# Narrow products of a decoder kernel padded to all 128 rows, and expert choice beside the scan split in two

## What is computed

```python
x = x + _L0_attn_ref(ln(x), ...)         # a scan over the 16 entries
x = x + _L0_xattn_ref(ln(x), ctx, mask)  # 16 heads of 8, 77 context rows
x = x + _L0_ffn_ref(ln(x), ...)          # router, top 2 of 8 experts, FF 512
x = x + _L1_attn_ref(ln(x), ...)         # self-attention with ALiBi
x = x + _L1_xattn_ref(ln(x), ctx, ctx, mask2, ...)
x = x + _L1_ffn_ref(ln(x), ...)          # top 2 of 8 again
```

```python
def step(params, x):
    z, y = x @ t_k.T, x @ t_v.T
    grads = grad(loss)(params, z, y)
    new = params - LR * grads
    return new, recon(new, x @ t_q.T)    # z + gelu(z W1' + b1) W2' + b2
```

## Time and profile before

| | |
|---|---|
| time, three runs | 741.73, 746.4, 748.1 us (median 746.4) |
| profiled execution | 753.57 us, of it a span of 751.5 us from first to last instruction |
| instructions | 18475 |
| PE busy | 603.6 us (80% of the span) |
| DVE, ACT, POOL busy | 483.9, 431.8, 359.0 us |
| granted TensorE clock, mean | 0.848 |

### The profile page before, as it was taken

One profiled execution on the slowest core, in us unless ns is written; L12 is line 12 of the kernel. 1 busy time (PEld: TensorE's weight loads), 2 busy tenths in 40 slices (PEclk: granted clock), 3 DMA queues, 4 the chain that ended last, 5 costly groups with the idle time before them and its releaser, 6 DMA issues.

```text
span 751.5 us, 18475 instructions
## 1 busy us (share of the span) xinstructions
PE 603.6 (80%) x6145; PEld 484.0 (64%) x6160; DVE 483.9 (64%) x1361; ACT 431.8 (57%) x897; POOL 359.0 (48%) x644
## 2 busy tenths in 40 slices
PE   2797999999999850999937999996997972499970
PEld 1485677777777640999924767664675651499970
DVE  7553545677767543555536999986898976255545
ACT  1452355778667311788814676765686751487840
POOL 5711332445467756466652433421445757365650
PEclk9996555989779565899968999999899996699995
DMA  7749950000000001222163000000000001222215
GB/s 193 231 168 321 330 196 1 2 2 3 1 15 16 22 22 46 72 73 71 52 216 160 2 2 3 1 3 1 2 3 8 28 19 47 53 72 69 68 37 167
DMA packets 41853, 52.59 MB, mean 70 GB/s; under 512 B 11056, under 2 KB 36897, under 8 KB 41473
## 3 DMA queue, kind: packets, MB, share of 16 engines
q1 hardware_dynamic: 37217, 42.07, 18.3%
q0 software_dynamic: 4544, 9.35, 3.8%
HBM read 40.97 MB, written 28.22 MB: 92 GB/s over the span
## 4 chain that ended last, share of the span: by engine, by line
issue 70%; PE 11%; POOL 6%; SPq 2%; DVE 2%; DMA 2%; POOLq 0%; DVEq 0%
PE p_s L1669 5%; POOL yo L1575 5%; PE p_o L1679 3%; PE p_in L1679 2%; DVE x L1626 2%; POOL to_row L1570 1%; SPq L1709 1%; PE p_pT L1661 1%; SPq L286 1%; DMA yo<-context,to_row 1%; DMA context<-xs 0%; DMA back<-yo 0%; SPq L1694 0%; SPq L1698 0%; POOLq L1569 0%
## 5 line engine op out<-in xcount | busy, mean ns | idle before, releaser
L1575 POOL DMA_INDIRECT yo<-context,to_row x78 | 76.1, 976 | 68.0 <-DVE context L1609 36.3
L1633 ACT ACTIVATE context<-pack 128x1156 f32 x78 | 90.6, 1166 | 30.8 <-DVE context L1609 13.4
L1669 PE MATMUL p_s<-xT_f,context 128*128 128x128 f32 x624 | 85.7, 282 | 0.0
L1669 PEld LDWEIGHTS p_s<-xT_f,context 128*128 128x128 f32 x624 | 79.2, 199 | 0.0
L1118 POOL DMA_INDIRECT xs<-send,x_index x64 | 64.1, 1001 | 23.9 <-issue 16.4
L1602 DVE TENSOR_SCALAR context<-p_s,context 128x128 f32<-128x128 f32 x156 | 47.5, 346 | 28.7 <-PE p_s L1669 23.8
L1312 ACT ACTIVATE x_pT<-p_pT 128x512 f32<-128x512 f32 (+1 forms) x96 | 48.8, 526 | 29.6 <-PE p_pT L1415 27.5
L1415 PE MATMUL p_pT<-sq,x_prob 128*128 128x128 f32 x320 | 59.7, 317 | 2.3 <-ACT x_pT L1312 1.6
L1640 ACT ACTIVATE context<-p_s,context 128x128 f32<-128x128 f32 x156 | 47.5, 356 | 21.4 <-PE p_s L1669 12.3
L1154 DVE TENSOR_REDUCE x_top<-p_s 128x12 f32<-128x924 f32 (+2 forms) x48 | 47.0, 1006 | 12.1 <-PE p_s L1401 12.0
L1164 DVE TENSOR_TENSOR x_prob<-p_s,x_top 128x768 f32<-128x768 f32 (+2 forms) x96 | 50.1, 577 | 0.1
(11 more groups left out here) (252 smaller groups left out, 1523.2 us busy)
## 6 DMA issues: line engine op xcount, KB each, us to landing
xs<-in_blank SPq DMA_DIRECT2D x2, 8707.5 KB, 43.3
pack<-in_pack SPq DMA_DIRECT2D x16, 578.0 KB, 8.5
context<-xs SPq DMA_DIRECT2D x78, 64.5 KB
back<-yo SPq DMA_DIRECT2D x16, 256.0 KB, 4.6
yo<-context,to_row POOLq DMA_INDIRECT x78
x<-in_x SPq DMA_DIRECT2D x4, 256.0 KB, 4.5
xs<-send,x_index POOLq DMA_INDIRECT x64
out<-x SPq DMA_DIRECT2D x4, 256.0 KB, 2.3
```

The source lines that it names most:

```text
L1575: nc.gpsimd.indirect_dma_start(yo[:, :], bass.IndirectOffsetOnAxis(to_row[:, n % NY, :], 0), y[:, n % NY, :], None).then_inc(y_stored[n % ...
L1633: nc.scalar.activation(ws[:, n % NW, :], pack[:, bass.ds(e, 1), :].rearrange("p a w -> p (a w)"), ACT.Copy).then_inc(ws_ready, 1)
L1669: ins = mm(p_h[n % 2][k // 2][:, P * (k % 2):P * (k % 2 + 1)], ws[:, n % NW, P * k:P * (k + 1)], xT[:, n % 2, :], start=True, stop=True)
```

## The change

Every narrow product above now contracts over 128 rows, with zeros in the rows that don't count. The ones come from the identity matrix or the triangular matrix `before`, whose column 0 or column 3 is broadcast to a 128x128 operand: one or three rows of ones over zeros. `scan_w2T`, `scan_b1r` and `bo_x0` come from an array `top_rows` that has the zeros already; `hT` and `hqT` are 128 rows high and set to zero once by POOL. The mask rows lie once instead of four times. Second, in the tables `choose` is cut in two, `max` goes ahead of it, `rank` and `address` move from lag 8 to lag 9, and `FIRST_SCATTER` goes from 2 to 3. Some waits of `rank` and `mix` follow that.

```diff
-    "out"), (0, "e_"), (7, "rturn"), (0, "dh"), (4, "tp2"), (8, "rank"), (2, "project"), (0, "g2"), (0, "g1"), (4, "mix"), (0, "g1b"), (7,
+    "out"), (0, "e_"), (7, "rturn"), (0, "dh"), (4, "tp2"), (9, "rank"), (2, "project"), (0, "g2"), (0, "g1"), (4, "mix"), (0, "g1b"), (7,
-FIRST_DVE = ((5, "scale"), (8, "choose"), (3, "max"), (0, "eTa"), (5, "res"), (1, "w2n"), (0, "slope2"), (0, "slope3"), (1, "comb"), (0,
-    "da"), (8, "address"), (3, "shift"), (1, "count"), (0, "w1n"), (5, "rcount"), (0, "b1n"), (0, "w2Tn"))
+FIRST_DVE = ((5, "scale"), (3, "max"), (8, "choose"), (0, "eTa"), (5, "res"), (1, "w2n"), (0, "slope2"), (0, "slope3"), (1, "comb"), (0,
+    "da"), (9, "address"), (3, "shift"), (8, "choose_next"), (1, "count"), (0, "w1n"), (5, "rcount"), (0, "b1n"), (0, "w2Tn"))
...
-FIRST_SCATTER = 2
+FIRST_SCATTER = 3
...
+        m["first_row"] = m["eye"][:, 0:1].to_broadcast([P, P])
...
-        m["scan_w2T"] = sb("scan_w2T", [HID + 1, P])
+        m["scan_w2T"] = sb("scan_w2T", [P, P])
-        m["scan_b1r"] = sb("scan_b1r", [1, HID])
+        m["scan_b1r"] = sb("scan_b1r", [P, HID])
...
                 pool.wait_ge(m["loaded_rest"], 16 * m["n_rest"])
-                pool.wait_ge(m["masks_placed"], 64 * NG)
+                for n in ("hT", "hqT"):
+                    nc.gpsimd.memset(m["scan_work"][n], 0.0).then_inc(m["scan_sems"]["set_up"], 1)
+                pool.wait_ge(m["scan_sems"]["set_up"], 2)
+                pool.wait_ge(m["masks_placed"], 64)
...
-                        for g in range(NG):
-                            r0 = STRIP * g
-                            sp.dma_start(m["mask_0"][r0:r0 + 1, :, :].rearrange("a b k -> a (b k)"), mk_0[:, :]).then_inc(m["masks_placed"], 16)
-                            for r in range(3):
-                                sp.dma_start(m["mask_1"][r0 + r:r0 + r + 1, :, :].rearrange("a b k -> a (b k)"),
-                                             mk_1[:, r, :]).then_inc(m["masks_placed"], 16)
+                        sp.dma_start(m["mask_0"][0:1, :, :].rearrange("a b k -> a (b k)"), mk_0[:, :]).then_inc(m["masks_placed"], 16)
+                        for r in range(3):
+                            sp.dma_start(m["mask_1"][r:r + 1, :, :].rearrange("a b k -> a (b k)"), mk_1[:, r, :]).then_inc(m["masks_placed"], 16)
...
-            mm(p_a, ones[0:1, :], b1r[:, :], start=False, stop=True).then_inc(a_ready, 1)
+            mm(p_a, m["first_row"], b1r[:, :], start=False, stop=True).then_inc(a_ready, 1)
...
+    if mask:
+        rows_on = (m["ident_bf"][:, 0:1] if mask_rows == 1 else m["before"][:, mask_rows:mask_rows + 1]).to_broadcast([P, P])
...
+        def choose(b, p):
...
+            best_of(s, g, 0)
+            if not beside:
+                choose_next(b, p)
+
+        def choose_next(b, p):
...
             s.done(nc.vector.scalar_tensor_tensor(lg[:, of, :], one_hot[:, 0, of, :], -3e38, lg[:, of, :], ALU.mult, ALU.add))
-            best_of(1)
+            best_of(s, g, 1)
             s.end()
...
-                    r = slice(STRIP * strip, STRIP * strip + mask_rows)
-                    mm(to.rearrange("p (h k) -> p h k", k=T), ones_bf[r, :],
-                       m[mask][r, b, :].unsqueeze(1).to_broadcast([mask_rows, len(hs), T]), start=True, stop=False)
+                    mm(to.rearrange("p (h k) -> p h k", k=T), rows_on,
+                       m[mask][:, b, :].unsqueeze(1).to_broadcast([P, len(hs), T]), start=True, stop=False)
...
-                wait(pe, row_read, FIRST_GROUP + groups_before(b - 3))
+                wait(pe, row_read, FIRST_GROUP + groups_before(b - (4 if beside else 3)))
...
-                mm(po_out, m["ones"][0:1, :], m["bo_x0"][0:1, :], start=False, stop=True).then_inc(projected_o, 1)
+                mm(po_out, m["first_row"], m["bo_x0"][:, :], start=False, stop=True).then_inc(projected_o, 1)
```

More of the change, by code:

```diff
@@ L49 @@
 CONTEXT_LOADS = 6
-SCAN_LOADS = 6
+SCAN_LOADS = 5
 EPS = 1e-5
@@ L467, in _ @@
                         lr = m["loaded_rest"]
-                        rest = [(m[f"bo_{n}"][:, :], t["rows"][ROWS.index(n + "_o"):ROWS.index(n + "_o") + 1, :].to_broadcast([P, P]))
-                                for n in ("x0", "s1")]
+                        rest = [(m["bo_x0"][:, :], t["top_rows"][:, 0:P]),
+                                (m["bo_s1"][:, :], t["rows"][ROWS.index("s1_o"):ROWS.index("s1_o") + 1, :].to_broadcast([P, P]))]
                         rest.append((m["bo_x1"][:, :], t["rows"][ROWS.index("x1_v"):ROWS.index("x1_v") + 1, :].to_broadcast([P, P])))
@@ L787, in b1n @@
             wait(dve, hqT_ready, b)
-            for w_, g_ in ((b1r[:, :], g_b1r), (b1c[:, :], g_b1c)):
+            for w_, g_ in ((b1r[0:1, :], g_b1r), (b1c[:, :], g_b1c)):
                 nc.vector.scalar_tensor_tensor(w_, g_, -GRAD, w_, ALU.mult, ALU.add).then_inc(b1_new, 1)
@@ L988, in attention @@
         heads = [(0, NH, HG, p_s[:, :, 0:GW].rearrange("p g (h k) -> p g h k", k=T))]
-        banks = [(range(HG * g, HG * (g + 1)), g) for g in range(NG)]
+        banks = [range(HG * g, HG * (g + 1)) for g in range(NG)]
         strips = [[(0, HG, g, 0)] for g in range(NG)]
@@ L1188, in route_count, with best_of, wide @@
             s.end()
+        def best_of(s, g, j):
+            of, n = of_group(g), GROUPS[g]
+            countdown = m["countdown"][:, :].unsqueeze(1).to_broadcast([P, n, NE])
+            hot = one_hot[:, j, of, :]
+            def wide(t):
+                return t.unsqueeze(2).to_broadcast([P, n, NE])
+            s.done(nc.vector.tensor_reduce(best[:, j, of], lg[:, of, :], AX.X, ALU.max))
+            s.done(nc.vector.tensor_tensor(hot, lg[:, of, :], wide(best[:, j, of]), ALU.is_equal))
+            s.done(nc.vector.tensor_tensor(hot, hot, countdown, ALU.mult))
+            s.done(nc.vector.tensor_reduce(where[:, j, of], hot, AX.X, ALU.max))
+            s.done(nc.vector.tensor_tensor(hot, countdown, wide(where[:, j, of]), ALU.is_equal))
         def choose(b, p):
@@ L1236, in vector @@
         if beside:
-            return dict(count=count_x, scale=scale_out, max=find_top, shift=shift, res=residual, rcount=route_count, choose=choose, address=address)
+            return dict(count=count_x, scale=scale_out, max=find_top, shift=shift, res=residual, rcount=route_count, choose=choose, choose_next=choose_next, address=address)
         if own:
```

53 lines of the change are left out of this document (25 added, 28 removed).

## The result

The changed kernel took 740.1 us (median of 16 runs, 736.07 to 744.58), the kernel before beside it 747.0 (16 runs, 741.73 to 757.22). The ratio is 0.9919, 95% interval 0.989 to 0.9947: 6.9 us off the median, where 12.4 were forecast. So the gain is 0.8 to 1.5%, and the two intervals barely touch: which gain one sees depends on the occasion too. A median is taken over all runs of a kernel, a ratio and its interval over the fast ones alone (within 1.5% of the fastest run of that kernel).

The account below looks back on a forecast made before the run. PE's two-speed clock was taken to set the scan's rounds. Terms -18.6 + 3.9 - 3.0 + 0.7 + 1.9 + 0.5 = -14.6 us took the profiled 753.6 to 739.0; the median forecast was 734, 8-in-10 range 724 to 748.

Parts of the forecast that it names:

- first rival: Clock doesn't heed the rows, so the five falls in the scan stay wherever they land: 746 us, chance 0.22.
- -18.6 + 3.9 - 3.0 + 0.7: x0, in us: five disturbed rounds freed; masks less mode changes over 13 rounds; reordered choice and rank; second half before w1n, b1n.
- second rival: The three early rounds before 107 us get the full clock too, losing 3 to 4 us each: 724 us, chance 0.08.
- Masks +0.4: x0: three mask products queue in one band instead of running in three, exposed between g1 and the next aT: +0.4 us per round.
- mode changes -0.1: x0: 0.9 us of PE's queue per round saved, but only 0.1 us shortens the round; the rest becomes waiting before g1.
- carrying over to the median: Step from the profiled execution (753.6 to 739.0 us) to a median run, 7.2 us lower: 731.8 carried over whole, 734 taken.
- hidden, so 0: x1: longer masks add 0.4 to 0.6 us per round on PE, hidden behind busy DVE; without cover up to 9.6 us.
- the signs named 5.3 us as the bound: What would show it: x1 rounds unchanged at 5.24 us if right, above 5.3 us if the third rival holds.
- third rival: PE becomes the bound of x1 if padded masks cost over 0.8 us, +0.6 us a round: 756 us, chance 0.10.
- choice and scatter: Reordered choice -3.0 us, its second half ahead of w1n and b1n +0.7, two more scatters in POOL's last burst +1.9.
- the start: Two more 128x128 memsets on POOL ahead of the scan's first product, which waits for POOL's set-up: +0.5 us.

Follow-up runs that it names:

- order_only: Kernel before with only the new order (max ahead of the choice in two halves, rank and scatters a round later), no padding: 749.4 us against 749.0.
- pad_only: Changed kernel with all padding but the order of the kernel before: 737.3 us, ratio 0.986 against the kernel before.
- changed_again: The changed kernel run once more, same program, on another occasion: 731.0 us against 743.9 for the kernel before, ratio 0.9855.
- x1_masks_in_bands: Changed kernel with x1's mask products over 3 rows in four bands as before: 735.6 us.
- choose_next_later: Changed kernel with the choice's second half moved to just before slope2 of the next round and rank just ahead of g1: 740.3 us, ratio 0.985.
- four_products_only: Kernel before with only a, po, eT and out padded to 128 rows, masks in bands, old order: 729.3 us, ratio 0.976.
- masks_in_bands: Changed kernel with x0's three mask products back to one row each in three bands: 727.6 us, ratio 0.973 against the kernel before.
- early_choice_all: Four products padded, both masks in bands, whole choice, rank and address in one round, second half before slope2, rank ahead of g1: 724.7 us.
- bands_eT_out_few: x0's masks in three bands as before, and eT and out over 33 rows again, a and po padded, against the changed kernel: median 741.7 us.

## Why the prediction was right and wrong

**Right: the clock.** PE's clock stays at 2.4 GHz from 101 to 193 us, and `order_only` and `pad_only` show that the padding did it. The first rival, by which the padding leaves the falls, is out. Whether it is the rows or the mode changes that the clock answers to wasn't taken apart. In `x0` the terms -18.6 + 3.9 - 3.0 + 0.7 summed to -17.0 and -18.5 were measured, in part by luck: 2.3 us came from the second round (14.65 to 12.33), which the prediction left as it was and whose clock rose at 101 us in this profile, but at 105 to 108 us in those of `changed_again`, `pad_only`, `x1_masks_in_bands` and `choose_next_later`, which have the same padding in `x0`. That is the second rival's gain, in part and by chance. In `order_only` PE was busy for 13.90 of 14.00 us in rounds at a clock of 0.63. The Trainium skill, "TensorE: Matmul & The Clock Gate", section "Why this matters for your kernels", puts a fall down to gaps between bursts; these rounds show 0.1 us of them. The bands of the masks are worth 0.44 us a round in `x0` and 0.2 in `x1`. The advice of the Trainium skill, "TensorE: Matmul & The Clock Gate", section "Why this matters for your kernels", to put narrow products side by side in distinct row groups, holds here for their time.

**Right: both costs per round.** Masks +0.4 (measured 0.44), mode changes -0.1 (measured 0.10), together rounds of 10.0 to 10.1 us (10.11). The rest of the mode changes came back as a longer wait ahead of `g1` (PEld waits 0.98 us in most rounds of the changed kernel, where about 1 was forecast; PE itself 0.7).

**Wrong: the carrying over to the median.** This is the step that failed: the share of the clock's gain that a median run keeps. "Carried over whole the sum gives 731.8; I take 734": of the 18.6 us of clock I let only 2.2 go. But the profiled execution of before was one of the slower draws of its kernel: 753.6 us against a median of 747.0 over 16 runs, which reach from 741.7 to 757.2 and of which 11 were faster than it. The changed kernel's profile (740.41) lies at its median. Measured profile against profile, the change was -13.2 us (forecast -14.6); of that, 6.6 us are the draw of before, 0.3 the other way that of the changed kernel, and -6.9 is what the medians showed. That the draws of before differ by their falls shows in its 17 runs beside `changed_again`: from 737.1 us at a mean clock of 0.861 to 759.8 us at 0.827. Where the gain is the removal of a disturbance that comes and goes, it has to be priced at its median number of occurrences. Three runs couldn't tell that number; the distance of 7.2 us between profile and median could have been taken off whole: 746.4 - 14.6 + 7.2 = 739.0, the profile's own result.

**Wrong: `x1` "hidden, so 0".** The step set the longer masks against 0.39 us of PE waiting, "plus about as much before `po`". The wait of 0.39 went first and then 0.2 us of each round was exposed: 3.6 us by `x1_masks_in_bands`, +2.8 against before, whose `x1` had 3.4 us more at 1.2 GHz. That the signs named 5.3 us as the bound was right; the third rival's mechanism came true at a third of its price (0.2 instead of 0.6 us a round).

**Right within the noise in their sum: choice and scatter.** Forecast -3.0 + 0.7 + 1.9 = -0.4; `order_only` has 1.004 (0.9996 to 1.0092), so nothing gained and up to 7 us lost. The round behind the first choice took 3.2 us more than its neighbours (13.31 against 10.1). That isn't to be held against the 0.7 forecast, which was the cost over the old order: in the old order the choice makes its round longer too, by 1.3 us at full clock (`four_products_only`, 11.02 against 9.68),

```profile
169.67:180.69 11.02, 8.86 (x112) 7.15 (x112) 10.03 (x42) 7.61 (x19) 4.66 (x9) 1.00 0.01 1
```

and about 3 us of the 13.31 lay at 1.2 GHz. What the new order itself added is at most the 1.9 us between them, less the price of that fall. I had overlooked that ACT's table load, before which ACT stands idle for at most 0.4 us in the other full rounds, comes behind the wait for the bias (2.19 us); and that `rank` in its new round waits for `add_out`. The later choice moved work from ahead of the last score to behind it and didn't save it. The burst took 2.2 us more (1.9 forecast).

**Not there: the start.** Forecast +0.5 for two more memsets; the scan's first product starts at 62.89 us instead of 62.93:

```profile
62.89 0.41 PE L848 MATMUL p_s<-back,scan_w1T 128*32 128x128 f32 x2 [4.14 <-POOL room_v L302]
```

**What I hadn't asked.** The change was costed as one block of padding. Each of its two parts alone buys most of the clock (the median clock of a run is 0.878 with the masks alone and 0.884 with the four products alone, 0.885 and 0.890 in the changed kernel, 0.851 to 0.855 before), so the second buys little: the four small products cost nothing, the masks 0.44 and 0.2 us a round. So the change gave away about 1 to 2%: `masks_in_bands` and `four_products_only` have 0.973 and 0.976, the changed kernel 0.992 and 0.9855.

## What to carry to other kernels

When a change removes a disturbance that isn't in every run, cost it against several runs' median count of it, and not against the one execution that the profiler caught. When it has several parts that may all work by one mechanism, price each alone: the cheap one may already do it. And a wait of an engine can hide added work only once: compare what is added with the smallest wait on the path around the cycle, and expect the rest to show.

## What the runs showed of the hardware

PE can fall to 1.2 GHz with a full queue: in `order_only` it was busy for 13.90 of 14.00 us in rounds at a clock of 0.63. Four products a round of 1 and 33 rows, 32 to 128 columns each, bear on that. Contracted over 128 rows with nothing else changed (`four_products_only`), they cost no time, and the falls ahead of the last score went from 7 to 17 us each to 3 to 4. The masks' products, with three times their columns, brought the clock up as well when they alone were padded (`masks_only`: none from 108 to 186 us, then 7 and 14 us), but at no gain in time. Padding does two things at once, it fills rows with zeros and it spares PE the changes between numbers of rows; what share each of the two has wasn't taken apart.

Which rounds fall isn't fixed: one program, `early_choice_all`, fell at 171, 178 and 226 us in one profile and at 183 and 224 us in the other (3 to 4 us each in the first, 3 and 24 us in the second), and `bands_eT_out_few` had its ten runs in three groups, near 730, 742 and 751.

Leaving and entering products of few rows costs 0.1 to 0.2 us of PE's queue each way: two-pass products of 128 columns went from 0.32 to 0.42 us each down to 0.22 to 0.23 when all had 128 rows.
